# Routed layers: the last two chunks' outputs stored tile by tile, token rows in partition order, and the state-space projections begun without a barrier

## The reference, cut to what matters

```python
def _moe_forward(x, wg, w1, b1, w2, b2):            # E = 8 experts, K = 2, H = 512
    cap = int(K * ((T + E - 1) // E))               # 1024 rows for each expert
    scores = softmax(xt @ wg); gates_k, idx_k = top_k(scores, K)
    ...                                             # loc: a row's place in its expert
    disp = zeros((E, cap, D)).at[idx_k, loc_c].add(contrib)
    h = relu(einsum('ecd,edh->ech', disp, w1) + b1)
    out = einsum('ech,ehd->ecd', h, w2) + b2
    y = einsum('tk,tkd->td', gates_k * valid, out[idx_k, loc_c])

def _mamba(x, W_in, conv_w, ...):
    u, z = split(x @ W_in, 2)
    uc = silu(conv_b + sum(up[:, k:k + T] * conv_w[:, k] for k in range(4)))
    ...                                             # projections, scan, z gate, W_out
x = x + 0.5 * _moe_forward(layernorm(x), ...)
x = x + _mamba(layernorm(x), ...)
x = x + 0.5 * _moe_forward(layernorm(x), ...)
```

## Time and profile before

| | |
|---|---|
| median of 3 runs | 2282.89 us (2281.88 to 2286.51) |
| the profiled execution, its own time | 2268.09 us |
| its span in the trace | 2266.2 us |
| PE busy | 1904.8 us (84%) |
| DVE, ACT, POOL busy | 1577.7 us, 1186.6 us, 1206.8 us |
| share of the chain that ended last, by engine | PE 48%, DVE 20%, issue 12%, POOL 12%, ACT 4%, DMA 3% |
| mean granted PE clock | 0.948 |

### The profile page before, as it was taken

One profiled execution on the slowest core, in us unless ns is written; L12 is line 12 of the kernel. 1 busy time (PEld: TensorE's weight loads), 2 busy tenths in 40 slices (PEclk: granted clock), 3 DMA queues, 4 the chain that ended last, 5 costly groups with the idle time before them and its releaser, 6 DMA issues.

```text
span 2266.2 us, 24220 instructions
## 1 busy us (share of the span) xinstructions
PE 1904.8 (84%) x6134; PEld 922.3 (41%) x6152; DVE 1577.7 (70%) x2040; ACT 1186.6 (52%) x2832; POOL 1206.8 (53%) x779
## 2 busy tenths in 40 slices
PE   4099677888888724977999899998987999999998
PEld 3077522333333513764333344443343433344443
DVE  7033486999999841328999866664797999955544
ACT  2322286555555341216999753432447999854332
POOL 4645103999999574543999600000885999800000
PEclk9999895999999966989999999999899999999999
DMA  8132382555545122334000000000741200000000
GB/s 263 58 88 90 104 137 98 175 172 175 177 168 177 69 68 62 96 109 120 0 0 0 1 1 1 0 0 19 192 133 34 60 0 0 0 1 10 5 9 14
DMA packets 108478, 163.50 MB, mean 72 GB/s; under 512 B 11144, under 2 KB 74051, under 8 KB 108273
## 3 DMA queue, kind: packets, MB, share of 16 engines
q1 hardware_dynamic: 100210, 146.29, 21.9%
q0 software_dynamic: 8192, 16.30, 2.1%
HBM read 124.97 MB, written 38.14 MB: 72 GB/s over the span
## 4 chain that ended last, share of the span: by engine, by line
PE 48%; DVE 20%; issue 12%; POOL 12%; ACT 4%; DMA 3%; POOLq 1%; DVEq 0%; SPq 0%; ACTq 0%
PE ps L1936 10%; PE ps L1909 10%; PE ps L1660 5%; PE ps L1670 5%; PE ps L1860 4%; PE ps L1851 3%; DVE arena L1406 3%; POOL slot_inputs L504 3%; DVE arena L1412 3%; DVE arena L1404 3%; PE ps L1786 2%; POOL arena L558 2%; DVE arena L1351 2%; PE ps L1910 2%; POOL arena L596 2%
## 5 line engine op out<-in xcount | busy, mean ns | idle before, releaser
L1909 PE MATMUL ps<-XT,c_phiT 128*128 (+1 forms) x512 | 264.9, 599 | 5.2 <-DVE arena L1444 3.9
L1860 PE MATMUL ps<-arena 128*128 128x512 f32 x512 | 250.6, 612 | 15.6 <-POOL arena L558 15.5
L566 POOL TENSOR_TENSOR arena<-arena 128x864 f32<-128x864 f32 x128 | 210.1, 1642 | 84.2 <-DVE arena L1404 81.5
L1851 PE MATMUL ps<-c_phiT,arena 128*128 128x512 f32 x512 | 244.7, 602 | 5.4 <-DVE arena L1406 2.3
L558 POOL TENSOR_TENSOR arena<-arena 128x1024 f32<-128x1024 f32 x128 | 246.6, 1928 | 0.0
L532 POOL TENSOR_TENSOR arena<-XT,arena 128x1024 f32<-128x1024 f32 x86 | 170.1, 2001 | 135.1 <-DMA arena<-input_gates 135.1
L1936 PE MATMUL ps<-arena 128*128 128x512 f32 x512 | 227.1, 603 | 11.1 <-DVE arena L1472 11.1
L596 POOL TENSOR_TENSOR arena<-arena 128x1024 f32<-128x1024 f32 x32 | 63.6, 2001 | 305.3 <-DMA arena<-value_rows 305.3
L1472 DVE TENSOR_TENSOR arena<-arena 128x4096 f32<-128x4096 f32 x32 | 140.2, 4422 | 121.0 <-ACT arena L903 121.0
L896 ACT ACTIVATE arena<-ps 128x512 f32<-128x512 f32 x256 | 151.2, 597 | 107.1 <-PE ps L1910 98.2
L514 POOL DMA_INDIRECT token_outputs<-arena x128 | 124.4, 972 | 149.7 <-DVE arena L1246 116.3
(11 more groups left out here) (229 smaller groups left out, 3586.9 us busy)
## 6 DMA issues: line engine op xcount, KB each, us to landing
arena<-input_gates SPq DMA_DIRECT2D x128, 512.0 KB, 3.9
arena<-value_rows SPq DMA_DIRECT2D x32, 512.0 KB, 5.0
arena<-slot_inputs SPq DMA_DIRECT2D x32, 258.0 KB, 2.8
arena<-in_L_ffn_w SPq DMA_DIRECT2D x32, 256.0 KB, 3.8
arena<-token_outputs SPq DMA_DIRECT2D x16, 512.0 KB, 7.4
slot_inputs<-arena SPq DMA_DIRECT2D x1, 4128.0 KB, 13.4
slot_inputs<-zero SPq DMA_DIRECT2D x1, 4128.0 KB, 33.4
token_outputs<-arena SPq DMA_DIRECT2D x1, 4096.0 KB, 17.7
```

Source lines behind the costliest of these rows:

```text
L566: pool.tensor_tensor(Ed[:, r, PSLOT * NA:].rearrange("p (n q) -> p n q", q=PSLOT), Lc[:, r, PSLOT * NA:].rearrange("p (n q) -> p n q", q=P ...
L1851: ins = pe.matmul(pbank(2 * h + c), xts[:, r // 2, :], phiT[:, at:at + CHUNK], start=True, stop=True)
L1860: ins = pe.matmul(pbank(4 + 2 * h + c), xns[:, r // 2, :], Dd[:, r, CHUNK * c:CHUNK * (c + 1)], start=start, stop=stop, skip_group_check=True)
L1909: pe.matmul(pbank(t % 4), phiT[:, P * t:P * (t + 1)], xt(b, c), start=True, stop=False)
```

## The change

- Chunks 14 and 15 of each routed layer put each of their four tiles in a PSUM bank of its own (`LAST_BANKS`); PE signals each tile, DVE adds the bias for each tile (`add_bias_by_tile`), and POOL waits for each tile. `done` turns chunk and tile numbers into semaphore values. POOL's last round of stores is written out behind its loop.
- Row numbers: tile t, partition p is stored at row pair 32 p + t, and a group's load takes one piece of 4 KB from each partition's rows.
- For m = 0 the barrier is left out on all five engines. PE makes the first piece's u between the sixth and the seventh `ln_turn`, ACT copies it and makes the first taps around its last two `XT` copies, and `ln_turn` uses bank 4. The rest of `project` waits for `gated` or for `ln_XT`.
- SP waits for the eighth `gated`, in place of the barrier, ahead of the two clears.

```diff
+        LAST_BANKS = [[pbank(i) for i in (6, 0, 1, 7)], [pbank(i) for i in (2, 3, 4, 5)]]
+        def done(m, c, j=0):
+            fine = 4 * E // 2 - 2
+            if isinstance(c, int) and c >= fine:
+                return (fine + 2 * PER_CHUNK) * m + fine + PER_CHUNK * (c - fine) + j + 1
+            return (fine + 2 * PER_CHUNK) * m + c + 1
@@ SP
-                yv = ytok[m].rearrange("(t p q) d -> p t q d", p=P, q=K)
+                yv = ytok[m].rearrange("(p t q) d -> p t q d", p=P, q=K)
-                stage_end(sp_, k + 1)
+                if m == 1:
+                    stage_end(sp_, k + 1)
             experts(0, 0)
+            sp_.wait_ge(sem("gated"), CHUNKS)
             clear(disp[1], "disp_zero")
@@ POOL
-                def store(i, first):
+                def store(i, first, last=False):
                     for r in range(YR):
-                        hold(pool, sem("y_out"), 16 * m + YR * i + r + 1)
+                        hold(pool, sem("y_out"), done(m, YR * i + r))
                         for j in range(PER_CHUNK):
+                            if last and r >= 2 and j:
+                                pool.wait_ge(sem("y_out"), done(m, YR * i + r, j))
@@ ACT
                 for c in range(CHUNKS):
                     ln_scale(n, c)
+                    if c == CHUNKS - 1 and m == 0:
+                        copy_u(0, 0, 0, True)
                     if c:
-                        ln_copies(n, (c - 1) // 2, (c - 1) % 2, 0)
-                ln_copies(n, BATCH - 1, 1, 0)
-                stage_end(act, k + 1)
+                        ln_copies(n, (c - 1) // 2, (c - 1) % 2, 4)
+                if m == 0:
+                    act.wait_ge(sem("prepared"), U_PADDED)
+                    first_taps(0, 0)
+                ln_copies(n, BATCH - 1, 1, 4)
@@ DVE
+                def add_bias_by_tile(n, r):
+                    for j in range(PER_CHUNK):
+                        dve.wait_ge(sem("l2"), done(m, n, j))
+                        dve.tensor_tensor(yo[:, r, j, :], LAST_BANKS[n % 2][j][:, 0:D], b2[:, E - 1, :], ALU.add)\
+                            .then_inc(sem("y_out"), 1)
-                add_bias(sbase + 15, 3, E - 1)
+                add_bias_by_tile(15, 3)
+                if m == 0:
+                    chain(dve.memset(u_pad[:, :, 0:CONV_PAD], 0.0))
+                    dve.nop().then_inc(sem("prepared"), 1)
@@ PE
                     for j in range(PER_CHUNK):
+                        if by_tile and j == PER_CHUNK - 1:
+                            pe.wait_ge(sem("y_out"), done(m, v - base - 1))
+                        y = LAST_BANKS[c][j][:, 0:D] if by_tile else pbank(6 + c)[:, P * j:P * (j + 1)]
                         for hb in range(HB):
-                            ins = pe.matmul(pbank(6 + c)[:, P * j:P * (j + 1)], hT[...], w2s[:, p, hb, :], ...)
+                            ins = pe.matmul(y, hT[...], w2s[:, p, hb, :], ...)
+                        if by_tile:
+                            ins.then_inc(sem("l2"), 1)
-                    ln_turn(2 * m + 1, c, c % 2, 0)
-                stage_end(pe, k + 1)
+                    ln_turn(2 * m + 1, c, c % 2, 4)
+                    if c == 5 and m == 0:
+                        pe.wait_ge(sem("ln_XT"), CHUNKS + 1)
+                        project_u(0, 0, 0)
@@ PE, project
+                    if first and h == 0:
+                        pe.wait_ge(sem("gated"), CHUNKS)
+                    else:
+                        if first:
+                            pe.wait_ge(sem("ln_XT"), 2 * CHUNKS)
+                        project_u(v, b, h)
@@ constants
-        "k_row_id": (K * np.arange(TOKENS).reshape(TILES, P).T + 1).astype(f),
+        "k_row_id": (K * np.arange(TOKENS).reshape(P, TILES) + 1).astype(f),
```

More of the change, by code:

```diff
@@ L517, in store @@
                                 .then_inc(sem(f"y_put{r}"), 16)
-                repeat(pool, E // 2, store)
-                stage_end(pool, k + 1)
+                store(0, True)
+                with pool.Fori(1, E // 2 - 1) as i:
+                    store(i, False)
+                store(E // 2 - 1, False, True)
+                if m == 1:
+                    stage_end(pool, k + 1)
             experts(0, 0)
@@ L657, in _, with copy_u, first_taps @@
             ln_copies(0, BATCH - 1, 1, 0)
+            def copy_u(v, b, h, first):
+                for d in range(DT):
+                    hold(act, sem("u_ps"), DT * v + d + 1)
+                    if h == 0 and not first:
+                        hold(act, sem(f"conv{d}"), v)
+                    act.activation(u_pad[:, d, CONV_PAD + CHUNK * h:CONV_PAD + CHUNK * (h + 1)], pbank(d), ACT.Copy)\
+                        .then_inc(sem("u_sb"), 1)
+            def first_taps(v, h):
+                for d in range(DT):
+                    hold(act, sem("u_sb"), DT * v + d + 1)
+                    if not below(v, 1):
+                        hold(act, sem("uc"), DT * (v - 1) + d + 1)
+                    act.activation(cacc[:, d, :], tap(d, h, 0), ACT.Copy, scale=conv_w[:, d, 0:1]).then_inc(sem(f"tap{d}"), 1)
             def experts(m, k):
@@ L711, in project @@
                     v = 2 * b + h
-                    for d in range(DT):
-                        hold(act, sem("u_ps"), DT * v + d + 1)
-                        if h == 0 and not first:
-                            hold(act, sem(f"conv{d}"), v)
-                        act.activation(u_pad[:, d, CONV_PAD + CHUNK * h:CONV_PAD + CHUNK * (h + 1)], pbank(d), ACT.Copy)\
-                            .then_inc(sem("u_sb"), 1)
-                    for d in range(DT):
-                        hold(act, sem("u_sb"), DT * v + d + 1)
-                        if not below(v, 1):
-                            hold(act, sem("uc"), DT * (v - 1) + d + 1)
-                        act.activation(cacc[:, d, :], tap(d, h, 0), ACT.Copy, scale=conv_w[:, d, 0:1]).then_inc(sem(f"tap{d}"), 1)
+                    if not (first and h == 0):
+                        copy_u(v, b, h, first)
+                        first_taps(v, h)
                     for d in range(DT):
@@ L1257, in chunks @@
                                               ALU.add, ALU.max).then_inc(sem("hT_dve"), 1)
-                        if not (first and r == 0):
-                            add_bias(v - 1, (r - 1) % YR, 2 * i + p if c == 1 else 2 * i + p - 1)
+                        if last and r == YR - 1:
+                            add_bias_by_tile(4 * i + r - 1, r - 1)
+                        elif not (first and r == 0):
+                            add_bias(4 * i + r - 1, (r - 1) % YR, 2 * i + p if c == 1 else 2 * i + p - 1)
                         if not (last and r == YR - 1):
@@ L1640, in xt, with project_u @@
                 return XT[:, ds(b, 1), CONV_PAD + CHUNK * h - shift:CONV_PAD + CHUNK * (h + 1) - shift].rearrange("p a t -> p (a t)")
+            def project_u(v, b, h):
+                for d in range(DT):
+                    if not below(v, 1):
+                        pe.wait_ge(sem("u_sb"), DT * (v - 1) + d + 1)
+                    pe.matmul(pbank(d), W_in[:, P * d:P * (d + 1)], xt(b, h), start=True, stop=True).then_inc(sem("u_ps"), 1)
             def experts(m, k):
@@ L1720, in project @@
                     v = 2 * b + h
-                    for d in range(DT):
-                        if not (first and h == 0):
-                            pe.wait_ge(sem("u_sb"), DT * (v - 1) + d + 1)
-                        pe.matmul(pbank(d), W_in[:, P * d:P * (d + 1)], xt(b, h), start=True, stop=True).then_inc(sem("u_ps"), 1)
+                    if first and h == 0:
[4 more added lines that the diff above has]
+                        project_u(v, b, h)
                     for d in range(DT):
```

31 lines of the change are left out of this document (17 added, 14 removed).

## The result

The change takes 2275.51 us (median of 7 executions, 2272.92 to 2277.12) beside 2283.55 us for the kernel before on the same chip (7 executions, 2281.88 to 2287.11): a ratio of 0.9960, 95% interval 0.9949 to 0.9972. That is 8.0 us less in medians and 9.1 by the ratio, where 9.1 were forecast (2273.8 us).

The account below looks back on a forecast made before the run. It took strict successions of engine waits at the three edited places as the bound. Tiles 1.8 and 1.9, rows 0.4 and barrier 5.0 sum to 9.1 us off the median 2282.89: 2273.8 us, range 2268 to 2280.

Parts of the forecast that it names:

- No barrier: Behind the first routed layer's normalisation, u and first taps are drawn forward and the convolution starts earlier: 5.0 us less.
- The 0.3 us that ACT was to lose: At the projections' start, ACT's Silu of the convolution comes late by 0.3 us, leaving 5.0 us of 5.3.
- Rows in partition order: First group loaded back at each routed layer's end lands 0.2 us sooner: 0.4 us less for both layers.
- The row that was also a load: Profile row of a 512 KB load, 4 KB to each partition, 3.7 us to landing, used to forecast the group's load.
- The fit in the Trainium skill: For the group's load, 2.0 us plus bytes over 436 GB/s: 3.2 us, 1.4 less for both layers; not in the sum.
- Stores tile by tile: In chunks 14 and 15, POOL's stores start earlier and wait for no tile: 1.8 and 1.9 us less in the layers.
- the added waits of POOL: Six waits ahead of stores whose tiles are long there, taken at nothing; at 0.1 us each, 0.6 us a layer.
- (A): PE's clock falls in the projections, 5.0 becomes 3.5: 2275.3 us; chance 0.82 together with the forecast.
- (B): Gain behind the barrier is hidden, as clears or `bvals` set the scan's start: 4.1 us less, 2278.8; chance 0.06.
- (C): Scattered stores become DMA-bound at each layer's end; at 1.9 us a store 6 us slower, 2288.8; chance 0.03.
- (D): Tiles do not help, as each added wait or semaphore hand-over costs: 5.0 + 0.4 left, 2277.5 us; chance 0.06.
- the earlier start of PE's full clock: In the weighing of the groups loaded back, a possible 0.7 us more gain, counted only in the best case.

Follow-up runs that it names:

- only_tile: The kernel before with only the tile-by-tile part (own banks, bias and waits by tile in chunks 14 and 15): 2283.49 us, ratio 0.9978.
- only_rows: The kernel before with only the order of the token rows changed, two lines: 2287.16 us, ratio 0.9993.
- only_barrier: The kernel before with only the barrier part (u and first taps inside the normalisation, bank 4, SP's wait for `gated`): 2282.35 us, ratio 0.9968.
- no_tile: The changed kernel without its tile-by-tile part, barrier part and row order kept: 2281.17 us, ratio 0.9962 of the kernel before.
- after_again: The change itself, unaltered, timed in a second session: 2273.56 us beside 2285.84 for the kernel before, ratio 0.9950.

## Why the prediction was right, and where it was not

The time was right (forecast 9.1 us, measured 9.1 and 11.4), but not by its own sum: that the two agree to a tenth is luck. One term of the sum was wrong by 3.7 us and more, and gains that it did not hold made up for it.

**No barrier: right.** Forecast 5.0, measured 28.04 - 22.47 = 5.6 between two points of DVE that enclose the place, and 6.1 against *only_tile* and *only_rows*, which keep the barrier. The order on ACT and PE, u in 1.88 us at clock 1.00, and the first tap ahead of the last copy all came. The 0.3 us that ACT was to lose did not: its Silu of the convolution starts 3.43 us behind DVE's first tap in both kernels (284.93 - 281.50, 286.11 - 282.68). As a whole *only_barrier* measured 7.3 with an interval of 4.3 to 10.3, which holds both.

**Rows in partition order: right.** Forecast 0.2 a layer, measured 0.27 and 0.26 (3.92 to 3.65 for the load; load to weighing 4.07 to 3.81 in the second layer). The row that was also a load, 3.7 us, was the right neighbour. The fit in the Trainium skill, page "DMA: Bandwidth & Descriptors", section "Anatomy of one DMA — SWDGE (gpsimd) path", gave 3.2 us; the page made it for transfers that GpSimd issues, and for this load, which SP issues, the trace does not agree, with 3.65.

**Stores tile by tile: wrong.** Forecast 1.8 and 1.9 us less, measured 0.5 and 0.2 more (0.2 and nothing against the kernels without the tile part). The step that failed is "the next tiles come every 0.91 us and POOL takes one every 1.276, so none is waited for". The tiles came so; the word of them did not. I took the hand-over from PE to DVE as constant, because every one in the trace of before was prompt, but those of chunks 14 and 15 fell into a rest of POOL or just behind it. The change removed that rest. With it fell the added waits of POOL, of which it says "I take them at nothing, since the cover is the lead of the tiles".

**The rivals.** (A) fell, the clock stayed. (B) fell: the clears start at 278.39 in the change, and from the first convolution to the scan it takes 96.40 us, against 97.14 before. (C) fell: POOL's pace stays at 1.28 us and the last store lands in 2.22. (D) is what happened, though not by a cost of each wait: its 2277.5 is the change without the tiles, and *no_tile* took about as long as the whole. But its gain of 5.4 us lies outside the interval measured, 6.4 to 11.6.

**What is left over.** The terms seen in the change's profile sum to 5.6 for the barrier, 2.3 for the stretch from the last store to the second addition (with the 0.5 of the loads) and 0.7 lost at the tiles: 7.2 us. For *after_again* they are 5.5, 1.2 and 0.7 lost, so 6.1. The runs measured 9.1 and 11.4. *no_tile* measured 8.7, with 5.5 for the barrier, nothing in all for the second term (0.2 lost, 0.2 won) and 0.5 lost at the stores, so 5.1 seen. Some 2 to 5 us of gain are thus unplaced. The profiles can't place them. The last stretch of the program differs by 4 between kernels that don't touch it, and by 2.5 between the two profiles of the change itself. The first layer's row stores take 2.7 longer in *no_tile* than in the change, though the two profiles of the change agree there to 0.1, so whether that follows the kernel or the execution stays open. Of the earlier start of PE's full clock the prediction had 0.7 in its range and nothing in its sum; the change's profile shows about 1.8 us less in that stretch in the two layers together, loads not counted. That the forecast met the median rests on these and not on its tiles.

## What to carry to other kernels

A hand-over that is prompt in a trace is prompt under the load of that moment. Before making it finer or moving it under another engine's unbroken work, ask what that engine was doing when the prompt ones were recorded. Where POOL stores indirectly without a pause and others wait for PE's word, one deliberate rest of 3 us can be cheaper than the 7 to 10 us that the late signals cost. And one profiled execution well under its median should be compared stretch by stretch with a second one before a sum is laid on it.

## What the runs showed of the hardware

PE's semaphore signals to DVE and to ACT arrived 1 to 11.6 us behind the recorded end of their matmuls while POOL issued indirect stores of 64 KB each 1.28 us without a rest. The earliest late one came in the fourth store of such a row. Others were prompt at the same point and later: the change's copy at 33.41, behind four stores of its row, and that of *after_again* at 806.05, behind nine. In chunk 15 the signals came through together once POOL paused: the last three biases start at 245.12 in one row, 0.8 us behind the end of POOL's store at 243.33. The copies at 45.55 and at 51.04 did not keep to that. Signals were prompt with no stores (0.04 us), and in or just behind a rest of 2 to 3 us. With the stores running, some were late in each profile in the row stores of both layers, except in the one of before, where 12 stores in a row delayed nothing, and in the two kernels with a rest; so by these runs unbroken stores are needed for it but don't suffice, and what else it takes stays open. So does whether PE's results themselves or only the signals are late, since the ends of matmuls are modelled in the profile.
